# Two transfers for the first pair's tokens, and a later place for the query weight's row

## The reference

```
xn = layernorm(x)
Q, K, V = xn @ Wq.T + bq, xn @ Wk.T + bk, xn @ Wv.T + bv
attn = softmax(Q K^T / sqrt(32)) V @ Wo.T + bo      # 16 keys for each query, see below
x = x + layernorm(attn)
x = x + layernorm(ffn(layernorm(x)))
```

## Time and profile before

| | us |
|---|---|
| median of 3 runs | 1690.47 |
| lowest and highest | 1690.1, 1692.84 |
| the profiled execution, its own time | 1692.04 |
| its span | 1690.2 |
| busy: TensorE | 1657.9 (98%) |
| busy: VectorE | 1309.7 (77%) |
| busy: ScalarE | 855.8 (51%) |
| busy: GpSimd | 1283.7 (76%) |

### The profile page before, as it was taken

One profiled execution on the slowest core, in us unless ns is written; L12 is line 12 of the kernel. 1 busy time (PEld: TensorE's weight loads), 2 busy tenths in 40 slices (PEclk: granted clock), 3 DMA queues, 4 the chain that ended last, 5 costly groups with the idle time before them and its releaser, 6 DMA issues.

```text
span 1690.2 us, 55468 instructions
## 1 busy us (share of the span) xinstructions
PE 1657.9 (98%) x22550; PEld 1321.3 (78%) x22550; DVE 1309.7 (77%) x2455; ACT 855.8 (51%) x1730; POOL 1283.7 (76%) x1303
## 2 busy tenths in 40 slices
PE   8999999999999999999999999999999999999994
PEld 6787777888777777877887877877888777778873
DVE  7677877877777778778778777787787787787777
ACT  4355555544544555555545445445555555454453
POOL 5577877778778778778777787787787787777867
PEclk9999999999999999999999999999999999999998
DMA  8566666666666656666766666666666666666653
GB/s 271 146 172 173 174 182 172 166 187 173 171 170 186 176 165 185 176 168 176 185 172 170 183 176 170 171 187 176 172 182 174 171 175 180 172 170 181 164 140 89
DMA packets 388635, 293.46 MB, mean 174 GB/s; under 512 B 296854, under 2 KB 296854, under 8 KB 388380
## 3 DMA queue, kind: packets, MB, share of 16 engines
q1 hardware_dynamic: 345552, 223.02, 50.0%
q10 hardware_dynamic: 42828, 66.90, 13.2%
HBM read 155.46 MB, written 67.24 MB: 132 GB/s over the span
## 4 chain that ended last, share of the span: by engine, by line
PE 90%; DVE 3%; ACT 2%; issue 2%; ACTq 2%; POOL 1%; DMA 0%; DVEq 0%; POOLq 0%
PE ps_k L1080 8%; PE ps_v L1081 6%; PE ps_v L1083 6%; PE ps_k L1081 6%; PE ps_v L1080 6%; PE ps_q L1081 6%; PE ps_q L1083 6%; PE ps_k L1083 6%; PE ps_q L1080 6%; PE ps_y L1160 6%; PE ps_y L1161 6%; PE ps_y L1164 6%; PE ps_s L1121 6%; PE ps_o L1140 5%; ACTq L943 1%
## 5 line engine op out<-in xcount | busy, mean ns | idle before, releaser
L910 ACT ACTIVATE q_sb<-ps_q,mr 128x512 f32<-128x512 f32 x127 | 87.4, 688 | 546.6 <-issue 541.5
L403 POOL TENSOR_TENSOR z<-z,b_row 128x512 f32<-128x512 f32 x124 | 187.5, 1531 | 224.3 <-DVE z L679 224.3
L605 DVE STREAM_TRANSPOSE qT<-q_sb 128x512 f32<-128x512 f32 x128 | 137.7, 1075 | 112.8 <-ACT q_sb L910 112.4
L1080 PE MATMUL ps_k<-wk_hi,xT_hi 128*128 128x512 f32 x504 | 212.3, 421 | 0.2 <-issue 0.2
L1081 PE MATMUL ps_k<-wk_lo,xT_hi 128*128 128x512 f32 x504 | 199.5, 396 | 1.2 <-issue 1.2
L1160 PE MATMUL ps_y<-wo_hi,oT_hi 128*128 128x512 f32 x504 | 199.1, 395 | 1.5 <-ACT oT_hi L926 1.5
L1161 PE MATMUL ps_y<-wo_lo,oT_hi 128*128 128x512 f32 x504 | 199.3, 395 | 0.0
L1081 PE MATMUL ps_q<-wq_lo,xT_hi 128*128 128x512 f32 x504 | 199.3, 395 | 0.0
L1081 PE MATMUL ps_v<-wv_lo,xT_hi 128*128 128x512 f32 x504 | 199.3, 395 | 0.0
L1080 PE MATMUL ps_q<-wq_hi,xT_hi 128*128 128x512 f32 x504 | 199.1, 395 | 0.0
L1080 PE MATMUL ps_v<-wv_hi,xT_hi 128*128 128x512 f32 x504 | 199.0, 395 | 0.0
(11 more groups left out here) (189 smaller groups left out, 3722.4 us busy)
## 6 DMA issues: line engine op xcount, KB each, us to landing
x_in<-in_xa SPq DMA_DIRECT2D x64, 512.0 KB, 5.2
x_t<-in_xt SPq DMA_DIRECT2D x64, 512.0 KB, 4.7
k_bd<-kT SPq DMA_DIRECT2D x512, 64.0 KB, 2.5
v_d<-v_tok ACTq DMA_DIRECT2D x128, 256.0 KB, 2.2
v_key<-v_d SPq DMA_DIRECT2D x128, 256.0 KB, 3.9
res<-in_xr SPq DMA_DIRECT2D x64, 512.0 KB, 5.3
p_bd<-pT ACTq DMA_DIRECT2D x508, 64.0 KB, 2.4
out<-o_sb SPq DMA_DIRECT2D x62, 512.0 KB, 2.9
```

The source lines that it names most:

```text
L403: nc.gpsimd.tensor_tensor(z[:, j, :], z[:, j, :], b_row[:, :], ALU.add).then_inc(z_done, 1)
L605: nc.vector.transpose(qT[t % 2][:, :, :].rearrange("p n h -> p h n"), q_sb[:, :].rearrange("p (h d) -> p h d", d=D)).then_inc(qT_done, 1)
L1080: nc.tensor.matmul(ps, x_hi[:, e, :], w_hi[:, e, :], start=e == 0, stop=False)
```

## The change

The first pair's tokens are loaded in two transfers, one for each tile of the pair, with a semaphore of its own for each: 256 KB, rows of 2 KB. The statistics of tile 0 wait for the first alone, those of tile 1 for the second. And spread("q") moves on TensorE from its place ahead of keys(0) to a place inside it: behind the first four products, ahead of the wait for xT_lo.

```diff
-        x_first = sem("x_first")
+        x_first = [sem(f"x_first{i}") for i in range(2)]
...
-            sp.dma_start(x_in[0][:, :, :], xa[0]).then_inc(x_first, DMA)
+            for j in range(2):
+                sp.dma_start(x_in[0][:, j, :], xa[0][:, j, :]).then_inc(x_first[j], DMA)
             load_half("k", wk, 0)
...
                 for j in range(2):
                     if v == 0:
-                        dve.wait_ge(x_first, DMA)
+                        dve.wait_ge(x_first[j], DMA)
                     nc.vector.bn_stats(st["X"][:, j, :], x_in[v % 2][:, j, :]).then_inc(stats_done["X"], 1)
...
                     for i, (x, w) in enumerate(((x_hi, w_hi), (x_lo, w_hi), (x_hi, w_lo))):
                         if i == 1:
+                            if k == "k":
+                                spread("q")
                             pe.wait_ge(first_low, 1)
...
             rows(0, (2, 3), ps_s[:, 1, :])
-            spread("q")
             keys(0)
```

## The result

The changed kernel takes 1695.2 us (median of 14 runs, 1691.53 to 1698.33) against 1690.51 us of the kernel before in the same series (14 runs). The ratio is 1.0023, with a 95% interval of 1.0016 to 1.003: 4.7 us slower by the medians and 3.9 by the ratio, where I had forecast +0.8 and a range that ended at 1693.2. The profiled execution has a span of 1696.5 us, 6.3 more than before. It is the slowest of the 14 (1698.33), so its trace may show more than the usual loss.

A forecast was written before the change was run, and what follows sets the result against it. The prediction took TensorE, busy 98% of the span, as the bound, with the start's lateness carried to the end. -0.57 + 2.00 us of slow work, weighed by the clock, gave 1690.47 + 0.8 = 1691.3 us; range 1689.6 to 1693.2.

The forecast's parts named there:

- the sum: Whole change: -0.57 + 2.00 us in slow work, weighed by the clock, gives +0.8 (0.5 to 1.3), so 1691.3.
- The first transfer in two: First tokens' load: one more issue leaves the key weights' landing where it was, cost 0, bound 0.43 us.
- the tokens' own gain: First statistics: 0.65 us earlier through the split, but worth 0 on the path to keys(0).
- the second half at 4.4: First tokens' load: first half lands at 3.7, second at 4.4, with 5.2 as the bound.
- The query row's spread: TensorE, first key products: keys(0) starts 0.57 us earlier, but the spread lies bare behind four products, +2.00 us.
- my 1.43: TensorE after the moved spread: 2.00 - 0.57 = 1.43 us behind, in work at the low clock.
- The clock: TensorE's first products: clock rises at 15.5 again, so 1.43 us of leftover work cost 0.8; rise at 14.9 gives 0.5.
- a rival: Late clock at the first products: rise at 18.8, +2.3, 1692.8, 25%; rise at 21.3 or later, 1693.9 and more, 4%.
- The price: First products: each microsecond of later clock rise costs 0.45 us; slow work done at the high level counts 0.233 / 0.425.
- The stall at 42.40: TensorE's 3.6 us wait at mixed(0): shifts whole, for 0; a rival had it shrink, down to 1686.1, 4%.

The follow-up runs named there:

- e1: Changed kernel with the query row's spread put back ahead of keys(0), so the two token transfers alone; ratio 1.0014 against the kernel before.
- e3: The changed kernel run again, nothing altered, for a second trace; ratio 1.0042 against the kernel before.
- e4: Changed kernel plus two unused products of 128 rows in TensorE's idle stretch ahead of keys(0); ratio 1.0017 against the kernel before.
- e8: Changed kernel plus two unused one-row products in TensorE's idle stretch ahead of keys(0); ratio 1.0018 against the kernel before.
- e13: Changed kernel with the four small loads for the queries' and values' rows issued behind the key weights' bias copy; one run, scores(0) +4.50 us.
- e5: Kernel before with the query row's spread moved as in the change, and the value row's spread behind keys(1); ratio 1.0019.
- e2: Kernel before with only the query row's spread moved behind the first four key products, tokens in one transfer; ratio 1.0014.
- e9: Kernel before plus one unused 2 KB load on SP between the tokens' transfer and the key weights' first half; ratio 0.9997.
- e12: The move of the query row's spread alone, against the kernel before, again for a second trace; one run, scores(0) +3.03 us.
- e14: Changed kernel with the key weights' first half issued between the tokens' two transfers; one run, scores(0) +5.09 us.
- e7: Kernel before with the query row's spread moved as in the change and one unused full-row product in its old place; ratio 0.999.
- e10: Kernel before with the first token buffer's rows 32 bytes apart, so its single transfer goes in packets of 2 KB; ratio 1.0004.
- e11: e7 again, for a second trace and more runs; ratio 0.9993 against the kernel before.
- e15: Kernel before, spread in its old place, plus one unused full-row product behind the first four key products; ratio 0.9997.
- e6: Kernel before with the first tokens in two transfers cut by partitions (64 rows of 4 KB each); ratio 1.0002.

## Why the prediction was wrong

The range ended at 1693.2, because the sum has the clock's rise at 15.5 as a fixed time and the split at nothing. Both failed; the clock is much the larger.

**The first transfer in two: "I take 0, and as the bound 0.43".** This step failed. even_out started 1.55 us later in the first trace and 1.9 to 2.9 in e1, e3, e4, e8 and e13 (of which some tenths are the early trace of before). I had reasoned in bytes: what lies ahead is the same, so an issue 0.4 us later doesn't matter. But the weights took 6.2 us from issue to landing instead of 5.1, with the engines at a share of 0.49. That part of the path costs 1.0 us at scores(5) in e1's trace and 0.14% by time. That the tokens' own gain is worth nothing on the path was right: the statistics started at 3.45 and keys(0) did not follow them. In my sum I also had the second half at 4.4; both were there by 4.1. The Trainium skill's rule that transfers should be large (DMA: Bandwidth & Descriptors, Rules for kernel authors) pointed to this side. The traces agree as to the sign, but the loss was not the halves' own rate; both halves were there 0.3 us before the whole would have been.

**The query row's spread: right.** The wait ahead of keys(0) was empty, the spread lay bare for 2.00 us, even_out("q") waited for it, and there was no wait behind the four products. With the weights late it cost more than my 1.43: in the old place it would have lain in the wait whole, as it does in e1 (8.00 to 10.07, keys(0) at 12.63).

**The clock: "If it rises at 15.5 again".** This step failed, and it is the one with the large price. I had the mechanism as a rival, with 25% for 16.5 to 20 and 4% for 21.3 and later; it rose at 27.94, 28.77 and 24.48 where the spread was moved (18.1 to 21.1 in the five others). The evidence stood in the earlier trace rows: from 4.33 to 10.98 TensorE was busy with one-row spreads and small products, and the clock didn't rise. I took one rise in one execution for a fixed time. The rival's own time, 4.5 us behind the spread's end, fits the five (3.0 to 4.4 us); why it was 9.2 to 11.9 us in the three others is not shown. That there the value row's spread came between the products a second time is a guess, as e5 does not test it. The price was right: with 0.55 for each microsecond of slow work and 0.45 for each of late clock, the measured 0.98 (start of the products) + 2.00 (spread) and 27.94 - 15.13 = 12.8 give 0.55 x 2.98 + 0.45 x 12.8 = 7.4; scores(0) was 7.69 late.

**The stall at 42.40: "it should shift whole, for 0".** Wrong as well, to the other side. Of 7.69 us, 3.18 went in the shorter stall and 1.06 in the clock that doesn't fall, and 1.68 came back as mixed(2)'s wait for v_key. The other traces agree: 5.68 became 2.96 in e2, 8.79 became 6.24 in e3. The 16 traces beside before fall into two groups. In the eight where the clock did not fall behind this stall (after, e2, e3, e8, e9, e12, e13, e14) 2.3 to 2.9 us of the lateness at scores(0) are gone at scores(5); in the eight where it fell again (e1, e4 to e7, e10, e11, e15) it is 0.8 at most. Seven of the first group are late by 3.0 us or more, and all of the second by less, but e9 with 1.26 is in the first: what shortens the stall was not tested.

**The sum.** +0.8 forecast; 5.14 in the first trace, of which the clock alone makes 0.45 x 12.8 = 5.8 ahead of what the stall gives back. By the times, 14 runs on either side, it is 3.9 to 4.7.

## What to carry to other kernels

While the clock is low, a product's price isn't its own duration only: ask what it does to the time at which the clock rises, and keep full-row products unbroken until then; a one-row product belongs ahead of them or in a wait. If an idle stretch is to be had ahead of the first dense products, a full-row product whose result nobody reads can be worth its place (e7 against e2); with the weights late it did not show in the times (e4 against e8). One rise in one trace is not a fixed time: take a second trace before you add it up. A split of an early load can move each later load's landing, and here neither the bytes ahead nor the issue time told by how much: look at the DMA share, and at the landing of what is third in the queue.

## What the hardware showed that I had not expected

- The clock's rise by the trace's clock record came 3.0 to 6.2 us into a stretch of key products, over all the traces but those with a full-row product ahead of them (e4, e7, e11: 1.7 to 3.3 us behind the start of that product, which follows small ones of 128 rows): 4.2 before (10.91 to 15.13), 6.2 after (21.78 to 27.94), 3.0 in e6 (12.12 to 15.11). In e9 the twelve key products from 11.26 to 16.8 ended without it, and it came at 17.40, in the spread behind. The same kernel differs from one execution to the next: 24.48 and 19.22 for the move alone. The Trainium skill (TensorE: Matmul & The Clock Gate, What's actually happening) has it that activity releases the gate; the traces agree for products of 128 rows; one-row products for 3.78 us in e8 did not do it.
- The key row and its bias, 2 KB each on ScalarE's queue, were used at 3.45 to 3.71 where the tokens were cut by tile, and at 4.33 to 5.18 in all other traces. It looks as if a small load comes after the large transfer that was issued beside it; that was not tested.
- SP's third large transfer landed at 7.5 to 9.2 us, with 0.5 MB ahead of it (after, e1, e3, e4, e6, e8, e13) as with 1.0 MB: 7.7 in before, and 7.7 to 8.3 in the eight other traces with one transfer.
